# Output bias in the value table, norm scalars split between VectorE and GpSimd, and shared weights loaded inside attention

## The reference, cut to what matters

```python
def xattn(x, context, tgt_mask, src_mask, Wq, Wk, Wv, Wo, bo):
    ...
    sim = einsum(q, k) * SCALE                  # 16 heads, 64 keys
    sim = where(tgt_mask == 0, neg, sim); sim = where(src_mask, sim, neg)
    out = einsum(softmax(sim), v)
    return einsum('bne,oe->bno', out, Wo) + bo

def ffn(x, gate_w, w1, b1, w2, b2, sw1, sb1, sw2, sb2):
    top1 = argmax(softmax(x @ gate_w.T))        # one of two experts for each row
    ...
    shared = relu(x @ sw1 + sb1) @ sw2 + sb2
    return routing_output + shared

x = x + xattn(layernorm(x), ...)                # x: 4 x 1024 x 512
x = x + ffn(layernorm(x), ...)
```

## Time and profile before

| | |
|---|---|
| median of 3 runs | 1966.02 us (1962.3 to 1966.55) |
| the profiled execution | 1961.06 us |
| its span | 1959.3 us |
| TensorE matmul busy | 1856.2 us (95%) |
| VectorE busy | 851.8 us (43%) |
| ScalarE busy | 835.5 us (43%) |
| GpSimd busy | 526.1 us (27%) |
| mean granted clock | 0.986 |

### The profile page before, as it was taken

One profiled execution on the slowest core, in us unless ns is written; L12 is line 12 of the kernel. 1 busy time (PEld: TensorE's weight loads), 2 busy tenths in 40 slices (PEclk: granted clock), 3 DMA queues, 4 the chain that ended last, 5 costly groups with the idle time before them and its releaser, 6 DMA issues. The chain is left out here.

```text
span 1959.3 us, 34126 instructions
## 1 busy us (share of the span) xinstructions
PE 1856.2 (95%) x11704; PEld 1170.5 (60%) x11705; DVE 851.8 (43%) x1571; ACT 835.5 (43%) x1473; POOL 526.1 (27%) x635
## 2 busy tenths in 40 slices
PE   8889989999779999999999999899999999999997
PEld 6344444444346666666666666566666666666664
DVE  6978778777624433444333333322222222222222
ACT  4654544455323333334544544333343333343333
POOL 1057777777600000100000100211212211212211
PEclk9999999999979999999999999999999999999998
DMA  9234433433382232223344465731121111121200
GB/s 319 76 90 121 125 118 120 131 112 108 108 283 76 76 102 82 97 87 106 118 145 144 140 225 184 240 84 44 49 61 48 55 43 40 47 60 46 62 23 15
DMA packets 186855, 206.00 MB, mean 105 GB/s; under 512 B 87568, under 2 KB 129040, under 8 KB 186384
## 3 DMA queue, kind: packets, MB, share of 16 engines
q1 hardware_dynamic: 178848, 179.66, 29.7%
q0 software_dynamic: 7920, 25.17, 4.1%
HBM read 129.56 MB, written 58.98 MB: 96 GB/s over the span
## 5 line engine op out<-in xcount | busy, mean ns | idle before, releaser
L975 PE MATMUL pH<-room_a,room_w 128*128 128x256 f16 (+1 forms) x6336 | 770.2, 272 | 11.7 <-DMA room_w<-s_split 8.7
L987 PE MATMUL pY<-room_w,room_a 128*128 128x512 f16 (+1 forms) x3120 | 756.7, 380 | 12.8 <-DVE room_a L1006 12.8
L975 PEld LDWEIGHTS pH<-room_a,room_w 128*128 (+1 forms) x6336 | 614.1, 98 | 192.6 <-issue 11.8
L1006 DVE TENSOR_TENSOR room_a<-room_a 128x256 f16<-128x256 f32 (+1 forms) x528 | 233.7, 443 | 911.6 <-ACT room_a L1000 909.3
L987 PEld LDWEIGHTS pY<-room_w,room_a 128*128 128x128 f16 x3120 | 305.6, 98 | 277.4 <-DVE room_a L1006 13.4
L998 ACT ACTIVATE room_a<-pH,e_bsel,sc 128x256 f32<-128x256 f32 (+1 forms) x272 | 152.0, 559 | 433.3 <-PE pH L975 408.3
L998 ACT ACTIVATE room_a<-pH,b1s,sc 128x256 f32<-128x256 f32 x256 | 144.4, 564 | 395.6 <-PE pH L975 395.6
L1172 POOL TENSOR_TENSOR room_a<-room_a,s_brow 128x512 f32<-128x512 f32 x32 | 42.4, 1348 | 600.9 <-DVE room_a L1014 600.9
L464 PE MATMUL pO<-room_w,room_b 128*128 (+1 forms) x768 | 174.3, 384 | 7.1 <-DVE room_b L690 7.1
L1000 ACT ACTIVATE room_a<-pH,e_bsel,sc 128x256 f16<-128x256 f32 (+1 forms) x272 | 149.7, 550 | 0.0
L1000 ACT ACTIVATE room_a<-pH,b1s,sc 128x256 f16<-128x256 f32 x256 | 142.4, 556 | 0.0
(11 more groups left out here) (182 smaller groups left out, 1476.9 us busy)
## 6 DMA issues: line engine op xcount, KB each, us to landing
s_er<-in_w SPq DMA_DIRECT2D x64, 512.0 KB, 5.1
room_w<-e_split SPq DMA_DIRECT2D x8, 2048.0 KB, 17.9
rows_room<-in_x SPq DMA_DIRECT2D x32, 256.0 KB, 2.7
room_a<-in_sw SPq DMA_DIRECT2D x32, 256.0 KB, 3.1
room_b<-in_x SPq DMA_DIRECT2D x32, 256.0 KB, 2.8
s_split<-room_a SPq DMA_DIRECT2D x64, 128.0 KB, 2.7
x_scratch<-room_b SPq DMA_DIRECT2D x32, 256.0 KB, 3.0
z_split<-room_b SPq DMA_DIRECT2D x32, 256.0 KB, 2.0
```

The lines of the kernel that those rows point to most:

```text
L975: mm = q.matmul(self.pH[j % 2][:, 0:rows], w[:, k, j * P:(j + 1) * P], zt[:, u, k, 0:rows], start=(n == 0), stop=(n == 3 * KC - 1))
L987: mm = q.matmul(self.pY[u][r][:, :], h[:, j % self.HR, r * P:(r + 1) * P], w[:, j, :], start=(j == 0 and n == 0), stop=(j == HC - 1 and n ...
L1006: q.tensor_tensor(self.hl[:, j % self.HR, 0:rows], self.hf[:, j % self.HR, 0:rows], self.hh[:, j % self.HR, 0:rows], ALU.subtract).then_in ...
```

## The change

1. `add_bo` is gone. The bias row `bo` is loaded before x, a row of 64 ones is made by GpSimd (`head0`), and each of the four batches' first value product gets a second matmul that adds `bo` to the 64 rows of the first head: as that head's probabilities sum to one, the output gets the bias. VectorE also takes the largest magnitude of `bo` and adds it to the scale's bound.
2. Norm scalars: GpSimd keeps one `pow` for each norm (`deviation`, `deviation2`). VectorE adds epsilon before it (`add_eps`, `add_eps2`, in front of `masked`) and makes the shift and the scaled deviation after it (`shifts`, `shifts2`, behind `gate`).
3. `lo_z`, the low half of z, moves from VectorE to the end of GpSimd's body, one body earlier.
4. SyncE loads all four quarters in `load_next`, and `load_next` stands at the head of body 31 in place of its end. After the barrier come `load_e(0)` and the bias row at once.

```diff
                         def body(g):
                             for u in range(N):
+                                if last_tile(g, u):
+                                    load_next()
                                 if not isinstance(g, int) or N * g + u + 6 >= N:
                                     step(sp, g, u, 6, load_x)
...
                                 step(sp, g, u, -2, store_z)
-                                if last_tile(g, u):
-                                    load_next()
...
                             sp.wait_ge(S["sim"], SUB)
-                            load_quarter(sp, wA, s1_d, s2_d, 0, 1, first_in["w1_in0"])
-                            load_quarter(sp, wA, s1_d, s2_d, 0, 2, first_in["w2_in0"])
+                            for q in range(QUARTERS):
+                                load_quarter(sp, wA, s1_d, s2_d, q, 1, first_in[f"w1_in{q}"])
+                                load_quarter(sp, wA, s1_d, s2_d, q, 2, first_in[f"w2_in{q}"])
...
                                 mm = pe.matmul(pk[n % 4], vd[:, q, b, :, :].rearrange("p h k -> p (h k)"),
-                                               wo_v[:, q, :], start=True, stop=True)
+                                               wo_v[:, q, :], start=True, stop=(q > 0))
+                                if q == 0:
+                                    mm = pe.matmul(pk[n % 4], head0, bob, start=False, stop=True)
...
+                        def deviation2(e, g, u):
+                            e.wait_ge(S["ve2"], count(g, u))
+                            at_least(e, S["pick1"], count(g, u) - 2)
+                            e.tensor_tensor(rsz[:, u % 2, :], ve2[:, u % 2, :], half[:, :], ALU.pow).then_inc(S["rs_z"], 1)
...
                                 step(pool, g, u, 2, negate)
                                 if not first_tile(g, u, 4):
-                                    step(pool, g, u, 4, rs_1)
-                                step(pool, g, u, -1, rs_2)
+                                    step(pool, g, u, 4, deviation)
+                                step(pool, g, u, -1, deviation2)
                                 step(pool, g, u, 1, norm)
                                 if not first_tile(g, u, 3):
                                     step(pool, g, u, 3, lo_x)
-                                step(pool, g, u, 0, add_bo)
                                 step(pool, g, u, 2, sub)
                                 step(pool, g, u, 2, low_w)
+                                step(pool, g, u, -1, lo_z)
...
+                        def add_eps2(e, g, u):
+                            e.wait_ge(S["agg2"], count(g, u))
+                            at_least(e, S["rs_z"], count(g, u) - 2)
+                            e.tensor_scalar(ve2[:, u % 2, :], mv2[:, u % 2, 1:2], EPS, None, ALU.add).then_inc(S["ve2"], 1)
...
+                        def shifts2(e, g, u):
+                            e.wait_ge(S["rs_z"], count(g, u))
+                            at_least(e, S["zh"], count(g, u) - 2)
+                            e.tensor_scalar(rs2[:, u % 2, :], rsz[:, u % 2, :], LN_SCALE, None, ALU.mult)
+                            e.scalar_tensor_tensor(out=shift2[:, u % 2, :], in0=mv2[:, u % 2, 0:1], scalar=-LN_SCALE, in1=rsz[:, u % 2, :],
+                                                   op0=ALU.mult, op1=ALU.mult).then_inc(S["rs2"], 1)
...
+                            if n == 27:
+                                largest(seen[:, SEEN_BO:SEEN_BO + 1], bob, bo_seen, in_bo)
...
                         link(dve.tensor_scalar(col(SV), amr[:, 2:3], amr[:, 3:4], float(DH), ALU.mult, ALU.mult))
+                        link(dve.tensor_tensor(col(SV), col(SV), seen[:, SEEN_BO:SEEN_BO + 1], ALU.add))
...
                                 aggregate(dve, 0, 0)
+                                add_eps(dve, 0, 0)
+                                shifts(dve, 0, 0)
...
                                 step(dve, g, u, -1, aggregate2)
+                                if not first_tile(g, u, 4):
+                                    step(dve, g, u, 4, add_eps)
+                                step(dve, g, u, -1, add_eps2)
...
                                 step(dve, g, u, 2, masked)
                                 step(dve, g, u, -1, agg2_done)
                                 step(dve, g, u, -1, gate)
+                                if not first_tile(g, u, 4):
+                                    step(dve, g, u, 4, shifts)
+                                step(dve, g, u, -1, shifts2)
                                 step(dve, g, u, -1, pick)
-                                step(dve, g, u, -2, lo_z)
...
-                for q in range(1, Q):
-                    load_quarter(sp, wA, s1_d, s2_d, q, 1, S[f"w1_in{q}"])
-                    load_quarter(sp, wA, s1_d, s2_d, q, 2, S[f"w2_in{q}"])
-                    if q == 1:
-                        sp.dma_start(brow[:, :], sb2.partition_broadcast(P)).then_inc(S["brow_in"], 16)
+                load_e(0)
+                sp.dma_start(brow[:, :], sb2.partition_broadcast(P)).then_inc(S["brow_in"], 16)
                 for u in range(2):
                     sp.wait_ge(stored["x1_out", u], 16 * SUB // 2)
                     sp.wait_ge(stored["z_out", u], 16 * SUB // 2)
                 load_r(0)
-                load_e(0)
```

More of the change, by code:

```diff
@@ L188, in xattn_ffn @@
         wB = weight_set(room_v)
-        first_in = {n: sem("s_" + n) for n in ("w1_in0", "w2_in0")}
+        first_in = {n: sem("s_" + n) for q in range(QUARTERS) for n in (f"w1_in{q}", f"w2_in{q}")}
         snet = Net("s", TILES, sem, sc, ident, A1, A2, room_a, rows_room, banks_a)
@@ L236, in xattn_ffn @@
                 sems("const_in", "src_neg", "stats", "rs", "xn", "xT", "xTh", "xTl", "sim", "drop", "neg", "smask", "mx", "sub", "exp",
[L237 removed]
+                     "sum", "rcp", "least_set", "half_set", "prob", "pT", "pTh", "pTl", "att", "x1", "stats2", "rs2", "z", "gd", "pick1",
                      "ve", "ve2", "agg", "agg2", "rs_x", "rs_z")
@@ L286, in xattn_ffn @@
                 mv2 = sb("mv2", [P, 2, 2], F32, a)
+                rs2 = sb("rs2", [P, 2, 1], F32, a)
+                rsz = sb("rsz", [P, 2, 1], F32, a)
+                ve = sb("ve", [P, 2, 1], F32, a)
                 ve2 = sb("ve2", [P, 2, 1], F32, a)
[L288 to L291, removed]
+                half = sb("half", [P, 1], F32, a)
                 shift1 = sb("shift1", [P, 2, 1], F32, a)
@@ L613, in _, with deviation @@
                         pool.partition_all_reduce(amr[:, 2:4], am[:, 2:4], P, RMAX).then_inc(reduced, 1)
[L614 to L628, removed]
-                                e.tensor_tensor(rs[:, u % 2, :], ve[:, u % 2, :], half[:, :], ALU.pow).then_inc(made_rs, 1)
-                                e.wait_ge(made_rs, count(g, u))
-                                e.tensor_tensor(shift[:, u % 2, :], minus_m[:, u % 2, :], rs[:, u % 2, :], ALU.mult).then_inc(done, 1)
-                            return fn
+                        def deviation(e, g, u):
+                            e.wait_ge(S["ve"], count(g, u))
+                            at_least(e, S["xn"], count(g, u) - 2)
+                            e.tensor_tensor(rs[:, u % 2, :], ve[:, u % 2, :], half[:, :], ALU.pow).then_inc(S["rs_x"], 1)
+                        def deviation2(e, g, u):
+                            e.wait_ge(S["ve2"], count(g, u))
+                            at_least(e, S["pick1"], count(g, u) - 2)
+                            e.tensor_tensor(rsz[:, u % 2, :], ve2[:, u % 2, :], half[:, :], ALU.pow).then_inc(S["rs_z"], 1)
                         def sub(e, g, u):
@@ L655, in negate, with lo_z @@
                             e.tensor_tensor(neg[:, u % 2, :], drop[:, u % 2, :], least, ALU.mult).then_inc(S["neg"], 1)
+                        def lo_z(e, g, u):
+                            e.wait_ge(S["zh"], count(g, u))
+                            e.tensor_tensor(zs[:, u % 2, DM:2 * DM], zf[:, u % 2, :], zs[:, u % 2, 0:DM], ALU.subtract).then_inc(S["z"], 1)
                         def low_w(e, g, u):
```

62 lines of the change are left out of this document (33 added, 29 removed).

## The result

The changed kernel takes 1970.78 us against 1963.2 for the kernel before on the same chip, nine runs of each. The ratio is 1.0034, with a 95% interval of 1.0024 to 1.0045: 4.7 to 8.8 us slower, 6.7 in the middle. The forecast's sign is right and its range holds the time; its +10.9 was too much, and its base too: it took 1966.0 from three runs of the kernel before, where nine give 1963.2, 2.8 us less. That 10.3 lies so near 10.9 is luck, as the table shows: two terms are off by +9.4 and -8.4.

What follows compares the result with a forecast made beforehand. The prediction took VectorE to bound the start and chains through GpSimd to hold attention at 13.20 us a tile. Terms 3.0 + 0.5 + 1.6 + 2.5 + 3.3 = +10.9 on 1966.0 gave 1976.9 us, range 1959 to 1986.

Steps and rivals of the forecast that it cites:

- Start: Before tile 0's masked scores: reduction of bo, an extra link, VectorE's power wait and bias matmuls add 3.0 us.
- Period: Attention's 24 periods: a loop from scores to scores of 13.22 us a tile against 13.20, +0.5 us.
- Seam: Attention to shared network: network starts 14.2 us later behind held stores, 10.9 given back afterwards, +3.3 us.
- Rival A: At the seam, stores are not held behind loads, so the network starts 3.3 us earlier; 1959.4 us, chance 0.13.
- Early tiles: Tiles 2 to 5 of attention take 38.4 us where they took 36.8, +1.6 us.
- tail: Last two tiles of attention, up to tile 31, take 26.3 us where they took 23.8, +2.5 us.
- Rival B: Attention's period falls to TensorE's 12.0 us as second norm needn't wait for same-body scores; 1938 us, half 1955; chance 0.07.
- D: Whole kernel: nothing measurable, as seam or edges come at their low ends and cancel the start; chance 0.10.
- C: Attention's period grows 0.4 us a tile because a later GpSimd norm delays VectorE's gate; +10, 1987 us, chance 0.12.

Runs made afterwards that it cites:

- x1: Changed kernel with the memsets of the row of ones moved behind GpSimd's first reduction over partitions; 1961.92 us, 0.9995 of the kernel before.
- y1: Kernel before plus a wait and one unused memset ahead of GpSimd's first reduction over partitions; 1971.13 us, ratio 1.0046.
- x4: Changed kernel with VectorE's gate moved behind the shifts; 1954.86 us, 0.9961 of the kernel before.
- y2: Changed kernel with shifts and shifts2 ahead of both the maximum and the gate; 1951.1 us, 0.9943 of the kernel before.
- x3: Changed kernel with all four quarters loaded before the barrier but behind the last body's stores; 1964.68 us, 1.001 of the kernel before.
- y3: Changed kernel with loads split: quarter 0 heading the last body, 1 and 2 behind tile 29's stores, 3 behind the barrier; 1953.69 us, 0.9959 of before.
- x2: Changed kernel with its weight loads put back as before, quarters 1 to 3 behind the barrier; 1961.27 us, 0.9993 of the kernel before.
- z1: Kernel before with only the change's weight loads, all four quarters at the head of body 31; 1971.67 us, ratio 1.0037.
- z3: Kernel before with only the bias folded into the value table, row behind the reduction, add_bo gone; 1951.37 us, ratio 0.9928.

## Why the prediction was right and wrong

The sign came out right and the size did not: +10.9 was forecast, +6.7 measured. Two steps failed. The period is the one that made the forecast too high, the start erred the other way and hid most of it.

- **Start, +3.0, in fact +12.4: a term put at nothing.** The terms I listed are borne out (x1: +3.4). What I left out is where the row's memsets stand: I costed them at nothing, since GpSimd idles there for 29 us, and didn't ask what else lies hidden in this idle time. 6.7 us of GpSimd standing did, and behind it 2.1 us of slower clock. x1 takes 9.0 off again by moving the memsets alone, and y1 puts 9.7 on the kernel before by adding them.
- **Period, +0.5, in fact -7.9: a term mis-sized.** The loop was right, and x4 and y2 show that `gate` and the maximum lie on it. Too large was `gate` to second norm, 1.37 for a measured 0.99 to 1.10: the small instructions are issued about 0.07 us apart (401.70, 401.77, 401.84), where I took the 0.1 to 0.2 of a chain of dependent links. Scores to scores is 12.87 and not 13.22, 0.33 a tile under the kernel before over 24 tiles. My bounds of 13.03 to 13.40 don't hold it, and the lower one doesn't follow from its own terms: four small instructions at 0.05 and a hop of 0.12 are 0.32 in place of 0.63, and with 3.9 for the last part the loop is 12.86.
- **Seam, +3.3 with both terms: right.** +13.9 and -10.8 against +14.2 and -10.9, and the steps behind M within 0.5 us. x3 and y3 show the cause, the order of stores behind loads in SyncE's queue; x2 and z1 show its worth, 8 and 7 us by the ratios (x2 against the changed kernel, z1 against the one before). That is more than the sum's 3.3, for two reasons that the profiles show. In x2 the network starts at M + 33.05, in the kernel before at M + 36.4: the other parts of the change had made the seam shorter, and the early loads used that up. In z1, where `lo_z` is still VectorE's, z(28) comes one body later, and the network starts 5.6 us later against M than in the changed kernel. Rival A had the wrong behaviour: the stores were held.
- **Early tiles +1.6 and tail +2.5.** The tail is 0.9 too large, as the new period is shorter than assumed. Tiles 2 to 5 rose by 0.2 in place of 1.6 for the same reason (11.66, 12.69 and 12.69 us, where I took 12.0, 13.2 and 13.2), and the row's +1.2 comes near my term by luck.
- **What the comparison hid:** z3 shows that the bias folding alone gives 14.1 us (11.4 to 16.9 by the ratio's interval; its profile lies 9.4 below that of before). From there to the changed kernel are 20.8 by the ratios. Undoing the early loads takes off 8 of them (x2) and moving the two memsets 7.7 (x1); the 5 left are the price of the new scalars' place and of `lo_z` on GpSimd together, which were not parted. x1's profile shows where they are lost against z3: 0.8 to M of tile 0, 1.7 to tile 5, 3.4 in the 24 periods, 1.7 to tile 31; 3.8 come back behind it (x2 against z3). I credited the folding with nothing, as I priced only the new loop.
- Rival B has the period fall, and it fell by 0.33 us a tile, but not for B's reason: the second norm does wait for the scores of its own body. D asked for ends that cancel, C for a later `norm`. Neither came. A slip in the chances: D and the rest of A are 0.14, not 0.13, which changes nothing.

**Open:** the period is 12.69 in the first tiles of the stretch and 12.81 to 13.01 later. The trace shows where it grows: from the end of `lo_x` to the scores 0.05 us pass at first and 0.18 to 0.29 later, from the shift's start to the second norm 0.19 and up to 0.29. Why is not known. Why z3's pace is 12.73, and what loop is second in x4, was read from waits and not tested. So was the 7 us that GpSimd stands after its third reduction, in both kernels (below).

## What to carry to other kernels

Idle time of an engine can hold work that the profile doesn't name, as the 28.94 us of GpSimd did here; when an instruction is put into it, ask which later one finds its preparation still to do, and put the new one behind that. A load that is brought forward in a queue is paid by the stores it passes: find who waits for them, and split the loads around them. When a change cuts one chain, write out the new loop instruction by instruction, then try its order: two VectorE instructions moved behind the shifts were worth 0.9% here, about as much as the folding itself (0.7%).

## What the runs showed of the hardware

- GpSimd's first reduction over partitions comes 6.74 us (after) and 6.75 us (y1) late with its operand ready, when it is reached late; if reached early, this lies in the idle time. A second gap of the same size, between GpSimd's memset at 107.88 and `lo_x` at 115.27 (before: 97.61 and 104.74), ends 0.25 and 0.71 us after its operand is there (115.02 and 104.03), where `lo_x` follows in 0.08 in attention. In the built programs an instruction that the profile doesn't show stands there too; it was not tested.
- Behind 6.64 us of idle TensorE the granted clock of after was 0.50 from 48 to 52 us, and the eight matmul records behind the gap took 2.2 us longer. With 0.31 and 0.77 us of idle time there (before, x1) it stayed at 1.00.
- Issue of 16 weight loads took 20.2 us with nothing between them, 1.44 us for each of the last ones (2.88 for two) and 0.55 for each of the first four. A store behind them landed some 7 us after issue.
- A one-column operation with two SBUF operands took 1.78 us beside a GpSimd operation. The timeline of after:

```profile
516.96 2.34 POOL L634 TENSOR_TENSOR room_b<-room_b 128x1024 f32<-128x1024 f32 x1 [0.48 <-DVE room_b L761]
517.53 1.78 DVE L719 SCALAR_TENSOR_TENSOR shift<-mv,rsz 128x1 f32<-128x1 f32 x1
```

  The same operation took 0.15 at 401.84. Its end (519.31) is that of GpSimd's `sub` (519.30), like `lo_z` before.
